# Attention of a gated two-layer block: ScalarE's subtraction ahead of its second exponential, scores ahead of the last turn, four input roundings on GpSimd

## The reference

```
x = x + tanh(g_xattn[0]) * L0_xattn(ctx, ctx, layernorm(x), kernel, D)   # long convolution
x = x + tanh(g_ffn[0])   * L0_ffn(layernorm(x), ...)                      # routed low-rank layer
x = x + tanh(g_xattn[1]) * L1_xattn(layernorm(x), ctx, ...)
x = x + tanh(g_ffn[1])   * L1_ffn(layernorm(x), ...)                      # 8 experts, top 2

def qdq(x):                       # along the last axis
    s = max(max|x| / 127, 1e-8)
    return clip(round(x / s), -127, 127) * s

def L1_xattn(x, cond):
    q = qdq(x) @ qdq(wq).T + bq
    k, v = split(cond @ wkv.T + bkv)
    attn = softmax(q k^T / sqrt(16))          # 16 heads
    return qdq(attn @ v) @ qdq(wp).T + bp
```

## Time and profile before

| | |
|---|---|
| three runs, median (lowest, highest) | 187.08 us (186.92, 187.10) |
| the profiled execution, its own time | 186.96 us |
| its span, first to last instruction | 185.0 us |
| mean granted TensorE clock | 0.997 |
| TensorE matmul busy | 169.5 us, 92% |
| VectorE busy | 151.6 us, 82% |
| ScalarE busy | 111.2 us, 60% |
| GpSimd busy | 102.7 us, 55% |

### The profile page before, as it was taken

One profiled execution on the slowest core, in us unless ns is written; L12 is line 12 of the kernel. 1 busy time (PEld: TensorE's weight loads), 2 busy tenths in 40 slices (PEclk: granted clock), 3 DMA queues, 4 the chain that ended last, 5 costly groups with the idle time before them and its releaser, 6 DMA issues.

```text
span 185.0 us, 3756 instructions
## 1 busy us (share of the span) xinstructions
PE 169.5 (92%) x1208; PEld 115.7 (63%) x1208; DVE 151.6 (82%) x455; ACT 111.2 (60%) x281; POOL 102.7 (55%) x177
## 2 busy tenths in 40 slices
PE   7989999998999999989768889889899899999991
PEld 7967666668565565555456666676578557656560
DVE  0799989985589989989998899999984897785663
ACT  2465044733432445764588999997799797574440
POOL 1079999996799431510295247565333569297000
PEclk9999999999999999999999999999999999999998
DMA  5979987100000000000000000000000079949943
GB/s 164 325 231 355 378 336 261 56 0 4 0 2 0 0 2 0 0 4 0 0 0 4 2 4 0 2 4 0 4 0 4 2 149 138 169 88 177 168 142 113
DMA packets 22771, 15.19 MB, mean 82 GB/s; under 512 B 17664, under 2 KB 21344, under 8 KB 22368
## 3 DMA queue, kind: packets, MB, share of 16 engines
q1 hardware_dynamic: 22112, 13.94, 29.6%
q10 hardware_dynamic: 640, 1.02, 1.5%
HBM read 9.68 MB, written 1.07 MB: 58 GB/s over the span
## 4 chain that ended last, share of the span: by engine, by line
PE 64%; ACT 15%; DVE 8%; DMA 5%; issue 4%; SPq 1%; DVEq 0%
PE PS L1843 9%; PE PS L1875 6%; PE PS L1473 5%; PE PS L1469 5%; PE PS L1470 5%; DMA CT<-ctxr 5%; ACT R L781 4%; ACT R L786 4%; PE PS L1574 4%; PE PS L1544 4%; PE PS L1671 4%; PE PS L1687 3%; PE PS L1508 3%; PE PS L1496 3%; PE PS L1657 2%
## 5 line engine op out<-in xcount | busy, mean ns | idle before, releaser
L1156 DVE TENSOR_REDUCE SM<-PS 128x8 f32<-128x1024 f32 x16 | 18.8, 1214 | 1.3 <-PE PS L1657 1.1
L357 POOL TENSOR_TENSOR R<-CT 128x512 f32<-128x512 f32 (+1 forms) x16 | 16.1, 1005 | 6.5 <-DMA CT<-ctxr 6.5
L573 POOL TENSOR_SCALAR R<-QT,SM 128x256 bf16<-128x256 f32 x32 | 15.9, 517 | 6.0 <-DVE SM L1235 5.7
L786 ACT ACTIVATE R<-PS 128x512 f32<-128x512 f32 x32 | 18.3, 604 | 0.8 <-PE PS L1671 0.7
L1671 PE MATMUL PS<-CON,R 128*128 128x128 f32 x128 | 18.3, 275 | 0.5 <-ACT R L786 0.5
L511 POOL TENSOR_TENSOR R<-R,ROW 128x256 f32<-128x256 f32 x8 | 5.8, 734 | 21.6 <-ACT R L723 10.9
L1357 DVE TENSOR_TENSOR R<-R,PS 128x512 bf16<-128x512 f32 (+1 forms) x17 | 11.6, 684 | 7.3 <-PE PS L1843 3.7
L582 POOL TENSOR_TENSOR R<-R 128x640 f32<-128x640 f32 (+1 forms) x12 | 15.0, 1282 | 2.8 <-DVE T_R L1081 2.8
L1671 PEld LDWEIGHTS PS<-CON,R 128*128 128x128 f32 x128 | 14.3, 140 | 2.1 <-issue 1.7
L920 ACT ACTIVATE R<-PS 128x512 f32<-128x512 f32 x17 | 10.1, 595 | 9.0 <-PE PS L1843 8.8
L1843 PE MATMUL PS<-R 128*128 128x512 bf16 x60 | 15.4, 379 | 0.0
(11 more groups left out here) (172 smaller groups left out, 452.4 us busy)
## 6 DMA issues: line engine op xcount, KB each, us to landing
WST<-w SPq DMA_DIRECT2D x3, 1024.0 KB, 11.8
T_R<-lagged SPq DMA_DIRECT2D x2, 768.0 KB, 8.2
X<-x SPq DMA_DIRECT2D x2, 512.0 KB, 4.8
CT<-ctxr SPq DMA_DIRECT2D x2, 512.0 KB, 8.1
y<-X SPq DMA_DIRECT2D x8, 128.0 KB, 1.8
WQP<-wqp ACTq DMA_DIRECT2D x1, 512.0 KB, 7.3
WKV<-wkv SPq DMA_DIRECT2D x1, 512.0 KB, 10.4
R<-sw SPq DMA_DIRECT2D x3, 128.0 KB, 3.4
```

Of the source, the lines that this page charges most:

```text
L357: return eng.tensor_tensor(KV[:, h % RING, lo:hi, 0:32].rearrange("p c (i j) -> p c i j", i=4), k[:, :, 0:4].unsqueeze(3).to_broadcast([P, ...
L573: nc.gpsimd.tensor_scalar(XB[:, u % XS, j, :], MX[:, b, :], GG[:, b, e:e + 1], 1.0, ALU.mult, ALU.mult).then_inc(e_xb, 1)
L786: nc.scalar.activation(ET[:, b % 2, 4 * k:4 * k + 4, :], PS[:, 4 + k % 2, :].rearrange("p (h n) -> p h n", h=4), ACT.Exp).then_inc(a_ex, 1)
L1156: V_.tensor_reduce(MX1[:, b % 2, 8 * c:8 * c + 8], S4[:, 8 * c:8 * c + 8, :], AX.X, ALU.max, negate=True).then_inc(a_mx, 1)
```

## The change

Four things. ScalarE's `a_last_subtract(s)` moves ahead of `a_exp(s-1, 1)`. TensorE's `a_scores(s+1)` moves ahead of `a_turn(s-1, 3)`. The rounding of the inputs of blocks 4 to 7 goes from ScalarE (`a_zq_`, behind the exponentials) to GpSimd (`a_round`, at the end of the loop body of b = 3 to 6), with a semaphore of its own, `a_zqp`, on which `a_transpose` and the later `rows` wait. `a_zq_` stays for blocks 0 to 3.

```diff
+            def a_round(b):
+
+                pool.wait_ge(a_z, AZT * (b + 1) - (b + 1 - GT))
+                pool.wait_ge(a_tr, b - 1)
+                nc.gpsimd.tensor_scalar(AT_[:, b % 2, :], AZ[:, b % 2, :], AR[:, b:b + 1], ROUND_H,
+                                        ALU.mult, ALU.add).then_inc(a_zqp, 1)
...
                 if b >= 4:
                     o_round(b - 4)
+                if 3 <= b < NB - 1:
+                    a_round(b + 1)
...
                 if s + 2 < NB:
                     a_q0_(s + 2)
                 if s >= 1:
+                    a_last_subtract(s)
                     a_exp(s - 1, 1)
-                if s >= 1:
-                    a_last_subtract(s)
...
-                if s + 3 < NB:
-                    a_zq_(s + 3)
+                if s == 0:
+                    a_zq_(GT - 1)
...
             def a_transpose(b):
-                pe.wait_ge(a_zq, b + 1)
+                if b < GT:
+                    pe.wait_ge(a_zq, b + 1)
+                else:
+                    pe.wait_ge(a_zqp, b - GT + 1)
...
                     a_turn(s - 1, 2)
-                    a_turn(s - 1, 3)
                 if s >= 1 and s + 1 < NB:
                     a_scores(s + 1)
+                if s >= 1:
+                    a_turn(s - 1, 3)
```

More of the change, by code:

```diff
@@ L305, in build @@
         o_qp = sem("o_qp")
+        a_zqp = sem("a_zqp")
         y_d, x3_d = sem("y_d"), sem("x3_d")
@@ L535, in rows @@
                 nc.gpsimd.tensor_scalar(NMR[:, b:b + 1], MV[:, b, 0:1], -1.0, None, ALU.mult).then_inc(a_zp, 1)
-                pool.wait_ge(a_zq, b - 1)
+                if b < GT + 2:
+                    pool.wait_ge(a_zq, b - 1)
+                else:
+                    pool.wait_ge(a_zqp, b - GT - 1)
                 pool.wait_ge(a_zp, 2 * (b - GT) + 1)
@@ L750, in a_zq_ @@
             def a_zq_(b):
-                act.wait_ge(a_z, AZT * (b + 1) - max(0, b + 1 - GT))
+                act.wait_ge(a_z, AZT * (b + 1))
                 if b >= 2:
```

## The result

| | before | changed |
|---|---|---|
| median of the runs on the same chip (lowest, highest) | 186.85 us (186.77, 187.10), 6 runs | 187.62 us (187.61, 187.78), 6 runs |
| the profiled execution, its own time | 186.96 us | 187.62 us |
| its span | 185.0 us | 185.8 us |
| ratio, with its 95% interval | | 1.0047 [1.0037, 1.0057] |
| first exponential of block 0 (stage 1) | 94.87 us | 94.66 us |

The changed kernel is slower by 0.8 to 0.9 us. The last rows say how to compare two traces of it: the first instruction that the change can reach came 0.21 us earlier in this execution, which has nothing to do with the change: 0.20 us of it stand in the traces already at 14 us, behind VectorE instructions that wait for a load (over all the traces of this case the first exponential lies between 94.66 and 95.18 us).

The account below looks back on a forecast made before the run. Bound taken: in the attention, the chain from ScalarE's subtraction through exponentials 2 and 3 to TensorE's values and next turn 0. 0 + 0.28 + 0.29 - 0.09 + 0.50 = +0.98 us, giving 188.1 us, range 187.2 to 188.6.

Parts of the forecast that it names:

- What closes a stage is not the scores.: Attention stages: exponential 3, then `o_ev_`, `o_project`, the last values and the next turn 0 close a stage; no size.
- Stages 1 to 3, "nothing": Exponential 3 ready 0.15 us before ScalarE reaches it, `a_rstd` giving the room; loop stays 6.47 us, so 0.
- Stages 4 and 5, +0.28 and +0.29: No `a_rstd` in stage 4; a later exponential 3 delays `o_ev_` and `o_project`: +0.28 us, then +0.57 in all.
- Stage 6, -0.09: Exponential 1's wait for `a_turn(5, 1)` goes, but exponential 3 comes later: sum falls to +0.48 us.
- Stage 7, +0.50: Subtraction goes ahead of exponential 1 with no scores to profit, delaying `a_turn(6, 3)` and what follows: +0.98 us in all.
- The rounding, 0: Moving four roundings from ScalarE to GpSimd costs and gains nothing: ScalarE's slots become idle time, GpSimd's work is covered.
- a lost cover: If GpSimd's rounding came late, `a_transpose` and TensorE behind it would be held up to 0.47 us in four stages.
- What follows passes it on: From `a_turn(7, 0)` to the first expert TensorE is busy 10.06 of 10.80 us, so all 0.98 us passes on.
- The scores' wait was the bound: Rival, attention: the six waits of 0.4 us set the pace; faster, 184.8 us, or weaker 186.6; chance 0.12.
- the sign named for it: Faster rival's test: whether exponential 3 still starts within 2.5 us of the subtraction's old start.
- No change: Rival: delays of stages 4 and 5 hidden, idle times in stages 6 and 7 absorb most: 187.2 us; chance 0.12.
- the port: Rival: each added GpSimd rounding holds VectorE 0.47 us through the shared ports, from stage 1 on: 188.5 us; chance 0.04.

Follow-up runs that it names:

- e5: The changed kernel with TensorE's order as before, so only ScalarE's subtraction moved, rounding on GpSimd: 188.72 us against 187.10 before, ratio 1.0091.
- e4: The changed kernel with the new orders of ScalarE and TensorE in stages 1 to 3 only: 186.72 us against 186.82 before, ratio 0.9997.
- e10: As e9, but with the new orders of ScalarE and TensorE in stages 1 to 3: 186.56 us against 186.74 before, ratio 0.9989.
- e7: The changed kernel with the new orders in stages 1, 2, 3 and 6 only: 186.73 us against 187.10 before, ratio 0.9980.
- e3: The changed kernel with ScalarE's second exponential ahead of the subtraction again in stage 7 only: 187.21 us against 186.82 before, ratio 1.0021.
- e1: The kernel before with only the rounding of blocks 4 to 7 moved to GpSimd: 186.86 us against 186.82 before, ratio 1.0002.
- e6: The changed kernel with ScalarE's order as before, so only TensorE's scores moved, rounding on GpSimd: 190.82 us against 187.10 before, ratio 1.0202.
- e8: As e4, plus TensorE's second turn ahead of `o_rows` in stages 6 and 7: 186.68 us against 187.10 before, ratio 0.9981.
- e2: The changed kernel with the rounding back on ScalarE, so only the two orders changed: 187.70 us against 186.82 before, ratio 1.0050.
- e9: As e1, with `a_rstd` of stages 1 to 3 moved behind the fourth exponential: 186.07 us against 186.74 before, ratio 0.9962.
- e11: As e9, plus the second turn ahead of `o_rows` in stages 6 and 7 and `o_y_` ahead of `m_rstd` in stage 7: 185.14 us, ratio 0.9913.
- e12: As e11, but with the rounding of blocks 4 to 7 on ScalarE behind `a_rstd`: 185.41 us against 186.74 before, ratio 0.9935.

## Why the prediction was right, point by point

**The time.** 188.1 us was forecast, from +0.98 us; measured are 187.62 and a ratio of 1.0047, which on 187.08 is +0.88. The attention is 0.94 us longer. The agreement is partly luck: 0.21 us that the forecast didn't have in stages 1 to 3 and 0.17 us too little in stage 7 nearly cancel, as the steps show:

| step | forecast, sum so far | trace, sum so far |
|---|---|---|
| stages 1 to 3 | 0 | -0.21 |
| stage 4 | +0.28 | +0.05 |
| stage 5 | +0.57 | +0.32 |
| stage 6 | +0.48 | +0.27 |
| stage 7, to `a_turn(7, 0)` | +0.98 | +0.94 |

(The trace's column compares the start of the next stage's first exponential, and for stage 7 that of `a_turn(7, 0)`, less 94.66 after and 94.87 before.)

**"What closes a stage is not the scores."** This premise holds for stages 1 to 3 and fails for stages 4 to 6. There the chain of the kernel before runs through the scores, and e5 shows it: scores that are 0.5 us later cost nothing in stages 1 and 2 and 0.49 us in each of stages 4 and 5. In stage 4 of the kernel before two paths meet at `o_project`. TensorE's list is the later one, but `o_ev_` ends only 0.07 us ahead of it (119.48 against 119.55). With the change the scores come 2.25 us behind the stage's first exponential (116.70 - 114.45) and not 2.81, so 0.56 us sooner. Nearly all of that goes to the fourth turn, whose slot of 0.49 us (117.78 to 118.27) now stands on the same path. The other path, through the fourth exponential, became 0.3 us longer and sets the stage. The sum came out because the two paths were that near to each other, which the prediction used (0.07 us) without saying which of them was the bound.

**Stages 1 to 3, "nothing".** Wrong by 0.07 us each. The prediction took the two slots for interchangeable, 0.50 for the exponential and 1.00 for the subtractions. But the subtraction follows the scaling `a_q0_` directly now, 102.02 - 101.65 = 0.37 us behind it, where the exponential stood 0.43 behind, and the next instruction follows the exponential after 0.48 (103.02 to 103.50). e4 has the same 0.24 us over three stages. The pitch is 6.40 us and not "still 6.47". The room that `a_rstd` gives is shown by e10: without it the fourth exponential waits.

**Stages 4 and 5, +0.28 and +0.29.** Right: +0.26 and +0.27, in part by two errors of 0.06 us that cancel. The 2.99 us from subtraction to fourth exponential measured 3.05, since the turn behind the scores has 0.69 us to its exponential (117.78 to 118.47) where the sum took 0.63; and the subtraction moved ahead by 0.56 us where the sum took 0.50. `o_project` shows the new wait of 0.28 us.

**Stage 6, -0.09.** Right within 0.04. The trade in it is shown by e7.

**Stage 7, +0.50.** It came out at +0.67. The step to the fourth turn, +1.11 forecast with all before it, was met to 0.02: 42.27 against 41.35 is +0.92, and +0.21 of stages 1 to 3 is the difference. `o_project` was met as well. What the forecast didn't have is 0.16 us ahead of `a_turn(7, 0)`. The reason given for the stage, the second exponential behind a subtraction that nobody waits for, is shown by e3, which takes only that back: the fourth turn is 0.66 us sooner and `o_project` 0.51. Without the 0.16 us the stage costs 0.51, and +0.50 was forecast. `a_turn(7, 0)` was named as the sign at "near 140.8"; it starts at 140.53, or 140.74 with the 0.21 us by which this execution was ahead at the first exponential.

**The rounding, 0.** Right, by e1. The range that was named for a lost cover was not tried: no run had the rounding late. The idle time ahead of the copy-out is 0.76 us and not 0.9, as in e1.

**What follows passes it on.** Right: the same 10.06 of 10.80 us.

**The rivals.** "The scores' wait was the bound" falls with the stages: the scores come 0.56 us sooner in stage 4 and the stage is 0.26 us longer. The waits view has the same, 0.6 us gone and 1.3 come further on. It had more for it than the prediction gave it, since the scores were on the chain in stages 4 to 6. And the sign named for it decides nothing: the prediction's own case puts the fourth exponential 118.89 - 116.40 = 2.49 us behind the subtraction's old place, within its 2.5; measured are 2.49 too (118.47 - 114.45, less the 1.53 us from the stage's first exponential to the old place). "No change" falls with e3: of the last stage's shift of 0.66 us at the fourth turn only 0.15 are taken up by `o_project`. For the port there is GpSimd's rounding of block 7 and VectorE's maxima beside it in the changed kernel:

```profile
118.31 2.32 DVE L1168 TENSOR_REDUCE SM<-PS 128x8 f32<-128x1024 f32 x2
...
118.33 0.48 POOL L549 TENSOR_SCALAR R<-R,SM 128x256 f32<-128x256 f32 x1 [0.46 <-DVE SM L1159]
```

The maxima took 2.32 us, as in the earlier trace rows, though the rounding started 0.02 us behind them. The Trainium skill ("SBUF — State Buffer", Who interferes with whom) itself exempts this case, a reduction, from its lock; the trace agrees with it, and where the rounding fell, no instruction that the page names stood beside it. Between 94 and 140 us no kind of VectorE instruction is longer in the changed kernel than before, by more than 0.01 us.

## What to carry to other kernels

Ask of each stage which instruction closes it, and not where the waits are: a wait that shows up in every stage (six times 0.4 us here) may be slack in some stages (1 and 2 here) and on the path in others (4 and 5), and taking it away is a loss where it pushes back another path that is nearly as late. The chain of waits has to be read for every kind of stage and not for one: the loop read from stages 2 and 3 was not that of stages 4 to 6. Two changes of order on two engines that are each bad alone (+1.7 and +3.9 us) may cancel to a small loss, so they have to be costed together, stage by stage, and the last stage by itself: it lost 0.5 us here, and what hurries the next block has no next block there. Work that is moved off an engine gives time only when something on the critical chain moves into the hole it leaves: here 0.01 us without, and 0.23 us with it (by one trace of each).

## What was unexpected in the hardware's behaviour

`a_turn(7, 0)` starts 0.49 to 0.50 us after the start of the transpose before it in some kernels (the changed one, e4, e6, e7, e8, e10) and 0.34 to 0.35 in the others (before, e1, e2, e3, e5, e9, e11, e12). There is one trace of each. The profile puts the gap down to "issue" and shows no semaphore that ends it. Ahead of this turn alone stand waits for the experts' weights, which had landed at about 34 us. e3 has the same instructions of TensorE in the same order as the changed kernel and not the gap. Timeline of TensorE in e4:

```profile
139.04 0.41 PE L1791 MATMUL PS<-CON,QT 128*128 128x128 f32 x2
139.53 1.07 PE L1689 MATMUL PS<-CON,R 128*128 128x128 f32 x8
```

and in e3:

```profile
139.72 0.41 PE L1791 MATMUL PS<-CON,QT 128*128 128x128 f32 x2
140.06 1.06 PE L1689 MATMUL PS<-CON,R 128*128 128x128 f32 x8
```

Its cause is open. It is 0.16 us of the 0.94.

The second thing lies behind the attention. At one place GpSimd scales a tile of 128x256 (L584) while VectorE adds two tiles of that size (L1351), and one of the two is held up by the other. Timeline of GpSimd and VectorE in e4, from 147.66 to 147.70 us:

```profile
147.63 0.47 POOL L584 TENSOR_SCALAR R<-QT,SM 128x256 bf16<-128x256 f32 x1
147.68 0.70 DVE L1351 TENSOR_TENSOR X<-T_R,R 128x256 f32<-128x256 f32 x1
```

and in e7, from 148.14 to 148.20 us:

```profile
148.12 0.73 POOL L584 TENSOR_SCALAR R<-QT,SM 128x256 bf16<-128x256 f32 x1
148.16 0.43 DVE L1351 TENSOR_TENSOR X<-T_R,R 128x256 f32<-128x256 f32 x1
```

GpSimd starts first both times, by 0.05 us in e4 and 0.04 in e7, and that small difference goes with which of them takes 0.26 us longer. Before, changed and e1 to e4 are as e4, e5 to e12 as e7. Where VectorE is the held one, the output projection before the experts stands 10.47 to 10.48 us behind `a_turn(7, 0)`, else 10.35 to 10.36: 0.11 us of the whole time. e5 to e12 ran on other chips than e1 to e4; whether the chip, the kernel or the moment decides is open. Nothing of this kind stands beside the roundings that the change moved.

The third thing is as small: on ScalarE a subtraction of 128x128 starts 0.37 us after the scaling before it (101.65 to 102.02 in the changed kernel), an exponential of 128x512 0.43 us after the same scaling (101.93 to 102.36 in the kernel before). So a slot can't be carried from one neighbour to another without looking.
